# An opening without cross-partition reductions on GpSimd, and with unread products of the identity on TensorE

## The chip, the core and the metric

The kernel runs on one core of a Trainium2 chip. The metric is the time on the device in microseconds; lower is better. One profiled execution of the kernel before gives every duration below.

## The reference

One transformer block with adaptive layer norm, on x of shape (2, 2048, 512):

```python
mod = (_silu(L0_c) @ L0_wmod).reshape(L0_c.shape[0], 6, 1, -1)
sa, ca, ga, sb, cb, gb = (mod[:, 0], mod[:, 1], mod[:, 2], mod[:, 3], mod[:, 4], mod[:, 5])
ga = (2 * (ga >= 0) - 1) * jnp.maximum(jnp.abs(ga), 0.25)      # gb likewise
h = _layernorm(x, axis=-1) * (1 + ca) + sa
x = x + ga * _L0_attn_ref(h, ...)     # linear attention: 16 heads of 32, elu(q)+1, elu(k)+1
h = _layernorm(x, axis=-1) * (1 + cb) + sb
x = x + gb * _L0_ffn_ref(h, ...)      # silu(gate) * up, 1376 wide; weights are lut[idx], 16 entries
return x
```

## The kernel before, in words

x is cut into 8 groups of 512 rows (4 tiles of 128). Every engine has its own instruction stream, in an order written out by hand, and the streams meet only in semaphores. A float32 operand of a big product is kept as two float16 parts, so that a product of 128x128 by 128x512 becomes three float16 products (`three`, L1128 to L1130). To cut a matrix so, the kernel needs its largest absolute value over all 128 partitions, rounded to a power of two: VectorE reduces along the columns (`absmax`, L765), GpSimd reduces over the partitions (`all_max` with `partition_all_reduce`, L456), and VectorE makes scales from it (`pow2`, `weight`, L757 to L780).

There are three parts. **Opening**: load x, the weights of k, v and q and the six slices of `wmod`; layer norm of group 0 (`norm` on GpSimd, L462 to L468, then ScalarE L687); the maxima `S_LUT`, `S_K`, `S_H1`, `S_V`, `S_Q`; `columns` (L1281) makes the scale and shift of a layer norm as columns, with 16 products of two columns for each slice; `row` (L1290) makes the four gates as full rows of 128 equal partitions; ScalarE writes h of group 0 in four chunks (L592, L593), and GpSimd its low part (L478). **Stages A**, 0 to 7, one for each group g, each of 12 steps o: q, k and v of group g on TensorE (`out_a`, 12 products for each step), the sums kv (`kv_a`, L1178), transposes of group g+1 (`xT_a`, L1136), and on VectorE, besides its part of all that, the look-up of feed-forward weights (`lookup`, L885 to L893), two wide units in stages 0, 2, 3 and 4 and one in stage 1. Stage 0 also has `h2_columns` and `h2_scales` at steps 3 and 5, with the maximum `S_H2`. Stages 6 and 7 build M, the product of the attention sums and the output weights, for batch 0, with the maximum `S_M0`. **Stages B**, 0 to 7: gate and up of the feed-forward, slot by slot (j from 0 to 10), with the attention output of the next group between; stage B1 builds M of batch 1 with the maximum `S_M1` (`m_max`, `m_scale`). In slot (0, 10) TensorE waits for `gu_ready`, which VectorE raises behind its last look-ups of stage B1 (L906). At the end come the eight groups' down products.

All loads go through the one queue of SyncE, in the order of the program.

Of the kernel before, what the change touches and what calls it, by code (L numbers as in the profile page):

```python
# [32 lines left out]
RMAX = bass.bass_isa.ReduceOp.max  # L33

P = 128
# [60 lines left out]
def adaln_kernel(nc, x, qwT, qb, kwT, kb, vwT, vb, owT, ob, lut, gateT, upT, downT, cT, wmod, out):  # L96
    with ExitStack() as ctx:
# [58 lines left out]
        silu_cr = hid_f[:, :, :].rearrange("p i (k m) -> p (i k) m", k=KC).rearrange("p (k b) m -> p k b m", k=KC)  # L156
# [15 lines left out]
        qn_f = sb("qn_f", [P, 2, GROUP], F32)  # L172
        kv = sb("kv", [P, BATCHES, KC, P + 1], F32)
# [15 lines left out]
        mods = part(look_flat, at + 16, F32, 4, KC, BATCHES)  # L189
# [20 lines left out]
        def sems(names):  # L210
# [3 lines left out]
        c_in, lut_in, rows_in = sems("c_in lut_in rows_in")  # L214
# [4 lines left out]
        consts, silu_done, rep_done, cols_done, rows_done, rows_read = sems(  # L219
            "consts silu_done rep_done cols_done rows_done rows_read")  # L220
        maxed, reduced, dve_step, pool_step, h1_ready, v_ready, q_ready, obga_ready, w_split = sems(
            "maxed reduced dve_step pool_step h1_ready v_ready q_ready obga_ready w_split")
# [62 lines left out]
        ROW_BANK, COL_BANK = (4, 5, 0, 1), (7, 0)  # L285
# [8 lines left out]
        def _(sp):  # L294
# [7 lines left out]
            load_mod(1)  # L302
            load_mod(0)
            sp.dma_start(xg[:, 0], xv[0]).then_inc(x_in[0], 16)
            sp.dma_start(raw[0], chunked(kwT)).then_inc(raw_in[0], 16)
            load_mod(2)
            sp.dma_start(raw[1], chunked(vwT)).then_inc(raw_in[1], 16)
            for row, src in ((kb_row[:], kb), (vb_row[:], vb), (obga[:, 0], ob), (obga[:, 1], ob)):
                sp.dma_start(row, src.partition_broadcast(P)).then_inc(rows_in, 16)
            sp.dma_start(qb_col, qb).then_inc(rows_in, 16)  # L310
            sp.dma_start(raw[2], chunked(qwT)).then_inc(raw_in[2], 16)
            load_mod(5)
            sp.dma_start(xg[:, 1], xv[1]).then_inc(x_in[1], 16)
            load_mod(4)
            load_mod(3)

# [6 lines left out]
            for i in range(3):  # L323
# [3 lines left out]
            sp.wait_ge(rows_done, 4)  # L327
            sp.wait_ge(cols_done, 2)
            sp.wait_ge(consts, 3)
            for j in range(6, FC):  # L330
                load_gate_up(j, idx_in[3])
            def stage_a(g, par, load):
# [94 lines left out]
        def _(pool):  # L427
# [4 lines left out]
            def link(ins):  # L432
# [5 lines left out]
            link(pool.memset(ident[:], 0.0))  # L438
            link(pool.affine_select(out=ident[:], in_=ident[:], compare_op=ALU.not_equal, fill=1.0, base=0,
                                    pattern=[[-1, P]], channel_multiplier=1))  # L440
            link(pool.memset(head_sum[:], 0.0))
            for i in range(P // HEAD):
                link(pool.memset(head_sum[HEAD * i:HEAD * i + HEAD, COPIES * i:COPIES * i + COPIES], 1.0))
            link(pool.memset(head_out[:], 0.0))
            for c in range(KC):
                link(pool.affine_select(out=head_out[:].rearrange("p (i d) -> p i d", d=HEAD), in_=head_out[:].rearrange("p (i d) -> p i d", d=HEAD),
# [986 lines left out]
```

## Time and profile before

| | |
|---|---|
| median of 3 runs | 1290.37 us (1290.29 to 1292.86) |
| the profiled execution | 1292.91 us, its span 1291.1 us |
| TensorE busy | 1188.0 us, 92% |
| VectorE busy | 745.4 us, 58% |
| ScalarE, GpSimd busy | 392.3 us (30%), 356.6 us (28%) |

The span is from the first to the last instruction; the execution's own time holds 1.8 us more that lie around it. Times in the rows below count from the start of the span.
### The profile page before, as it was taken

To read this page: it belongs to the slowest core of one execution; us is meant where nothing else is said; L and a number is where in the kernel's file an instruction comes from. 1 tells how busy PE (TensorE), PEld (TensorE's weight loads), DVE (VectorE), ACT (ScalarE), POOL (GpSimd) and SP (SyncE) were. 2 spreads that over 40 slices of the span, in tenths; PEclk is the share of its full clock that TensorE was granted. 3 is DMA by queue.
4 is the path that set the end of the run, shared out by engine and by line. 5 is a ranking of instruction groups with operands and counts; after the bars stand their busy time and mean duration, and the time that the engine had idled before them with its cause. 6 is when DMAs were issued, how large, how long until landed. Compare 5 with 4: busy or idle time off the path is not lost.

```text
span 1291.1 us, 14367 instructions
## 1 busy us (share of the span) xinstructions
PE 1188.0 (92%) x5528; PEld 569.4 (44%) x5528; DVE 745.4 (58%) x1106; ACT 392.3 (30%) x608; POOL 356.6 (28%) x344
## 2 busy tenths in 40 slices
PE   4499699889999798796999999999999999999998
PEld 4255345444554343342444444444444444444443
DVE  2449789998856467976788698987621110010010
ACT  0224355645663532313233242433223210000000
POOL 1101000000030533525355263644523221111111
PEclk9889899999999899898999999999999999999999
DMA  9413111121201342121032131212121244444441
GB/s 326 130 33 110 66 65 35 64 98 66 74 25 65 119 165 99 57 90 66 29 107 80 66 106 72 77 69 106 39 106 48 77 179 153 153 153 153 153 153 65
DMA packets 52229, 125.79 MB, mean 97 GB/s; under 512 B 5216, under 2 KB 15456, under 8 KB 47040
## 3 DMA queue, kind: packets, MB, share of 16 engines
q1 hardware_dynamic: 52160, 124.87, 27.7%
q8 instruction: 43, 0.70, 0.2%
q14 instruction: 26, 0.21, 0.0%
HBM read 77.15 MB, written 47.71 MB: 97 GB/s over the span
## 4 chain that ended last, share of the span: by engine, by line
PE 64%; DVE 16%; issue 11%; ACT 4%; POOL 4%; DMA 1%; POOLq 0%; SPq 0%; DVEq 0%; ACTq 0%
PE bank L1128 20%; PE bank L1129 20%; PE bank L1130 20%; DVE look_buf L893 3%; DVE w_ffn L893 2%; DVE look_buf L890 1%; DVE arena L890 1%; PE bank L1247 1%; PE bank L1136 1%; DVE qp L921 1%; DVE shared L912 1%; ACT h L592 1%; ACT h_f L593 1%; DMA xg<-in_x 1%; PE bank L1281 1%
## 5 line engine op out<-in xcount | busy, mean ns | idle before, releaser
L1128 PE MATMUL bank<-h,w_ffn 128*128 128x512 f16 (+1 forms) x528 | 203.3, 385 | 23.8 <-DVEq L906 12.5
L1129 PE MATMUL bank<-h,w_ffn 128*128 128x512 f16 (+1 forms) x528 | 202.8, 384 | 0.0
L1130 PE MATMUL bank<-h,w_ffn 128*128 128x512 f16 (+1 forms) x528 | 202.4, 383 | 0.0
L544 POOL TENSOR_TENSOR shared<-hid_f,shared 128x512 f16<-128x512 f32 (+1 forms) x88 | 112.7, 1281 | 311.8 <-ACT shared L716 311.8
L1062 DVE SCALAR_TENSOR_TENSOR hid_f<-bank,sc,shared 128x512 f32<-128x512 f32 (+1 forms) x88 | 65.8, 748 | 151.2 <-PE bank L1130 114.1
L1069 DVE SCALAR_TENSOR_TENSOR shared<-bank,sc,gb_row 128x512 f32<-128x512 f32 x32 | 24.0, 751 | 215.6 <-PE bank L1130 215.6
L1128 PE MATMUL bank<-w_ffn 128*128 128x512 f16 (+1 forms) x352 | 136.3, 387 | 0.9 <-DVE hid_f L1062 0.9
L716 ACT ACTIVATE shared<-hid_f 128x512 f16<-128x512 f32 (+1 forms) x88 | 55.4, 630 | 267.1 <-DVE hid_f L1062 267.1
L1129 PE MATMUL bank<-w_ffn 128*128 128x512 f16 (+1 forms) x352 | 136.2, 387 | 0.0
L1130 PE MATMUL bank<-w_ffn 128*128 128x512 f16 (+1 forms) x352 | 136.2, 387 | 0.0
L1128 PE MATMUL bank<-arena,h 128*128 128x512 f16 x256 | 101.4, 396 | 7.9 <-issue 6.5
L1129 PE MATMUL bank<-arena,h 128*128 128x512 f16 x256 | 100.9, 394 | 0.0
L1130 PE MATMUL bank<-arena,h 128*128 128x512 f16 x256 | 100.8, 394 | 0.0
L709 ACT ACTIVATE shared<-bank,sc 128x512 f32<-128x512 f32 (+1 forms) x88 | 60.3, 685 | 127.7 <-PE bank L1130 127.7
L890 DVE TENSOR_SCALAR look_buf<-look_buf,tab_x,tab 128x512 uint32<-128x512 uint32 x133 | 98.1, 767 | 0.8
L1128 PEld LDWEIGHTS bank<-h,w_ffn 128*128 128x128 f16 (+1 forms) x528 | 53.4, 101 | 95.9 <-issue 18.5
L581 POOL TENSOR_TENSOR xg<-xg,shared 128x512 f32<-128x512 f32 x32 | 41.0, 1280 | 198.1 <-DVE shared L1069 198.1
L1130 PEld LDWEIGHTS bank<-h,w_ffn 128*128 128x128 f16 (+1 forms) x528 | 53.6, 102 | 62.8 <-issue 3.1
L462 POOL TENSOR_SCALAR sc<-mv 128x4 f32<-128x4 f32 x16 | 6.6, 410 | 266.7 <-DVE mv L803 146.4
L1129 PEld LDWEIGHTS bank<-h,w_ffn 128*128 128x128 f16 (+1 forms) x528 | 53.5, 101 | 58.7 <-issue 2.4
L893 DVE COPY_PREDICATED look_buf<-look_buf 128x512 uint32<-128x512 uint32 x76 | 71.7, 944 | 1.1
L1128 PE MATMUL bank<-arena,w_ffn 128*128 128x512 f16 (+1 forms) x176 | 66.8, 379 | 0.0
(183 smaller groups left out, 2029.5 us busy)
## 6 DMA issues: line engine op xcount, KB each, us to landing
hid_dram<-shared SPq DMA_DIRECT2D x80, 256.0 KB, 2.0
w_ffn<-hid_dram SPq DMA_DIRECT2D x8, 2560.0 KB, 9.6
xg<-in_x SPq DMA_DIRECT2D x16, 1024.0 KB, 7.2
qp_dram<-qp SPq DMA_DIRECT2D x8, 1024.0 KB, 4.9
x_dram<-xg SPq DMA_DIRECT2D x8, 1024.0 KB, 4.1
xg<-x_dram SPq DMA_DIRECT2D x8, 1024.0 KB, 4.8
out<-xg SPq DMA_DIRECT2D x7, 1024.0 KB, 11.4
qp<-qp_dram SPq DMA_DIRECT2D x6, 1024.0 KB, 5.2
```

Source lines behind the costliest of these rows:

```text
L544: pool.tensor_tensor(hid[0:m, e % HIDS, 1], hid_f[0:m, e % 2], hid[0:m, e % HIDS, 0], ALU.subtract).then_inc(hid_done, 1)
L581: pool.tensor_tensor(xg[:, par, t], xg[:, par, t], y_t[:, t % 2], ALU.add).then_inc(y_done, 1)
L592: act.activation(dst[:, 0, c], bank[c % 2][:], ACT.Identity, bias=bias, scale=scale)
L709: act.activation(silu_g[0:m, e % 2], bank[2 + 2 * (e % 2)][0:m], ACT.Silu, scale=c1(C_INV_G)[0:m]).then_inc(silu_g_done, 1)
L716: act.activation(hid[0:m, e % HIDS, 0], hid_f[0:m, e % 2], ACT.Copy).then_inc(hid_hi_done, 1)
L890: ins = dve.tensor_scalar(buf(dst), buf("m0"), tab_x[:, a:a + 1], tab[:, 2 * a:2 * a + 1], ALU.bitwise_and, ALU.bitwise_xor)
L893: ins = dve.copy_predicated(buf(dst), buf(a), buf(b))
L1062: dve.scalar_tensor_tensor(hid_f[0:m, i], bank[3 + 2 * i][0:m], c1(C_HID)[0:m], silu_g[0:m, i], ALU.mult, ALU.mult).then_inc(hid_f_done, 1)
L1069: dve.scalar_tensor_tensor(y_t[:, t % 2], bank[2 + t][:], c1(C_INV_D), gb_row[:, g // PER_BATCH], ALU.mult, ALU.mult).then_inc(y_read, 1)
L1128: pe.matmul(dst, a_hi, b_hi, start=first, stop=False)
L1129: pe.matmul(dst, a_hi, b_lo, start=False, stop=False)
L1130: last = pe.matmul(dst, a_lo, b_hi, start=False, stop=end)
```

## The change

GpSimd makes no reduction over partitions any more. In its place (`all_max` on TensorE) one product with the identity spreads the 128 per-partition maxima over a PSUM tile, and VectorE reduces it (`amax`). The maximum of the look-up table, which is the same on every partition, needs neither.

The scale and shift of a layer norm come as rows: `small_rows` runs products of 32 weight columns in strips of the array, `mod_turn` transposes the result. The gates are made in stage A1 (`g_rows`, then `row`), not in the opening. The loads have a new order: x of group 0, the weights of k, `wmod` slices 1 and 0, the weights of v and q; look-up indices are loaded between the later slices. Stage A0 takes its transposes two steps later (`M_LATE`). The first step of stage A0 waits for h chunk by chunk. `kv` is cleared by GpSimd, and `m_scale(1)` stands three slots earlier. Last, `fill` issues products of the identity with itself, into a bank that nobody reads before it is overwritten: 64 at the very start, 8 before `mod_turn(0)`, 8 before stage A0.

```diff
+            sp.dma_start(xg[:, 0], xv[0]).then_inc(x_in[0], 16)
+            sp.dma_start(raw[0], chunked(kwT)).then_inc(raw_in[0], 16)
+            load_mod(1)
+            load_mod(0)
+            sp.dma_start(raw[1], chunked(vwT)).then_inc(raw_in[1], 16)
+            sp.dma_start(raw[2], chunked(qwT)).then_inc(raw_in[2], 16)
+            load_row(kb_row[:], kb).then_inc(rows_in, 16)
+            sp.dma_start(qb_col, qb).then_inc(rows_in, 16)
+            load_two(0)
+            sp.dma_start(xg[:, 1], xv[1]).then_inc(x_in[1], 16)
+            load_mod(4)
+            load_mod(3)
+            load_two(1)
+            load_mod(2)
+            load_mod(5)
+            load_two(2)
+            load_row(vb_row[:], vb).then_inc(late_in, 16)
+            for b in range(BATCHES):
+                load_row(obga[:, b], ob).then_inc(late_in, 16)
+            sp.wait_ge(mrows_done, 1)
+            for j in range(6, FC - 1):
                 load_gate_up(j, idx_in[3])
+
...
+                if g == 1:
+                    sp.wait_ge(g_done, 1)
+                    sp.wait_ge(consts, 3)
+                    load_gate_up(FC - 1, idx_in[3])
...
-            def all_max(n, count):
-
-                pool.wait_ge(maxed, count)
-                pool.partition_all_reduce(c1(C_AMAX + n), c1(C_MAX + n), P, RMAX).then_inc(reduced, 1)
-                pool.wait_ge(reduced, count)
...
+            link(pool.memset(kv[:].rearrange("p b k n -> p (b k n)"), 0.0))
...
+            norm(0, stats_done, ve_done, rstd_done, nmr_done)
+            link(pool.memset(head_out[:], 0.0))
...
-            all_max(S_LUT, 1)
-            norm(0, stats_done, ve_done, rstd_done, nmr_done)
-            all_max(S_K, 2)
-            all_max(S_H1, 3)
-            all_max(S_V, 4)
             for c in range(KC):
                 h_lo_a(0, 0, c)
-            pool.wait_ge(h_done, 8)
-            all_max(S_Q, 5)
-
-            def h2_max():
-                pool.wait_ge(xn_done, 4 * 1 + 4)
-                all_max(S_H2, 6)
...
+            def amax(n, count, src):
+
+                dve.wait_ge(reduced, count)
+                dve.tensor_reduce(c1(C_AMAX + n), src, AX.X, ALU.max).then_inc(amax_done, 1)
+                dve.wait_ge(amax_done, count)
+
             def weight(i, n, count, col):
 
 
-                dve.wait_ge(reduced, count)
+                amax(n, count, bank[6][:, 0:P])
...
+            def mod_rows(i, n):
+
+                rows = 2 * HEAD
+                dve.wait_ge(mrows_done, i + 1)
+                dve.tensor_scalar(mod_row[i][0:rows], bank[MROW_BANK[i]][0:rows], head_sum[0:rows, 0:1], None, ALU.add).then_inc(mrow_done, 1)
+                dve.wait_ge(mrow_done, i + 1)
+                dve.tensor_reduce(c1(C_MAX + n)[0:rows], mod_row[i][0:rows], AX.X, ALU.max, apply_absolute_value=True).then_inc(maxed, 1)
...
-            stage_a(0, 0, True, LOOK_A[0], {3: [h2_columns], 5: [h2_scales]})
+            stage_a(0, 0, True, LOOK_A[0], {4: [lambda: mod_rows(1, S_H2)], 5: [h2_scales]}, M_LATE)
...
-                        8: [lambda: m_scale(1)], 9: [lambda: m_cut(1, 0), lambda: m_cut(1, 1)],
+                        5: [lambda: m_scale(1)], 9: [lambda: m_cut(1, 0), lambda: m_cut(1, 1)],
...
+                if g == 0 and o == 0:
+                    for k, pair in enumerate(pairs):
+                        pe.wait_ge(h_done, 4 + k + 1)
+                        last = three(bank[2][:], [pair], k == 0, k == KC - 1)
+                    last.then_inc(proj_done, 1)
+                else:
+                    three(bank[2 + o % 4][:], pairs).then_inc(proj_done, 1)
...
+                if c == 0 and n == 2:
+                    pe.wait_ge(amax_done, N_M1)
...
+            def all_max(count, n, dst, rows=P):
+
+                pe.wait_ge(maxed, count)
+                pe.matmul(dst, c1(C_MAX + n)[0:rows].to_broadcast([rows, P]), ident[0:rows, 0:rows], start=True, stop=True).then_inc(reduced, 1)
+
+            def small_rows(dst, tiles, done):
+
+                for k in range(KC):
+                    for i, (weights, m) in enumerate(tiles):
+                        if k == 0:
+                            pe.wait_ge(mod_in[m], 16)
+                        last = pe.matmul(dst[HEAD * i:HEAD * i + HEAD], weights(k), mod_raw[m][:, k], start=(k == 0), stop=(k == KC - 1),
+                                         tile_position=(0, HEAD * i), skip_group_check=True)
+                last.then_inc(done, 1)
...
+            def mod_turn(i):
+                rows = 2 * HEAD
+                pe.wait_ge(mrow_done, i + 1)
                 for c in range(KC):
...
+                    last = pe.transpose(bank[MCOL_BANK[i]][:, c * rows:(c + 1) * rows], mod_row[i][0:rows, c * P:(c + 1) * P], ident[0:rows, 0:rows])
+                last.then_inc(mcols_done, 1)
...
+            def g_rows():
+                pe.wait_ge(h_f_done, 4 + 3 + 4)
+                small_rows(bank[0], [(lambda k, b=b: silu_r[:, k * BATCHES + b], m) for m in (2, 5) for b in range(BATCHES)], g_done)
...
+                pe.matmul(bank[(i + 1) % 2][:], head_out[rows], g_row[rows], start=True, stop=True,
+                          tile_position=(HEAD * i, 0)).then_inc(rows_done, 1)
...
+            def fill(n):
+
+                for _ in range(n):
+                    pe.matmul(bank[3][:, 0:P], ident[:], ident[:], start=True, stop=True)
+
             pe.wait_ge(pool_step, 2)
+            fill(64)
+            all_max(N_K, S_K, bank[6][:, 0:P])
+            pe.wait_ge(rep_done, 2)
+            mod_rows(0, 1, 0)
             xT_a(0, 0, 0)
             xT_a(0, 0, 1)
-            pe.wait_ge(rep_done, BATCHES * KC)
-            row(0, 2)
+            fill(8)
+            mod_turn(0)
+            mod_max(0, N_H1, S_H1)
             xT_a(0, 0, 2)
+            all_max(N_V, S_V, bank[6][:, 0:P])
             xT_a(0, 0, 3)
-            row(1, 2)
-
...
+            fill(8)
+
+            def h2_rows():
+                pe.wait_ge(h_f_done, 4 + 3)
+                mod_rows(1, 4, 3)
+
+            def h2_turn():
+                pe.wait_ge(h_f_done, 4 + 4)
+                mod_turn(1)
+                mod_max(1, N_H2, S_H2)
+
+            stage_a(0, 0, True, {3: [h2_rows], 5: [h2_turn]}, M_LATE, first=True)
+            pe.wait_ge(pool_step, 10 + P // HEAD)
+            stage_a(1, 1, True, {0: [g_rows], 2: [lambda: row(0), lambda: row(1)], 3: [lambda: row(2), lambda: row(3)]})
...
-                    {2: [lambda: m_turn(1)], 4: [lambda: m_prod(1, 2), lambda: m_prod(1, 3)]})
+                    {2: [lambda: m_turn(1)], 4: [lambda: m_prod(1, 2), lambda: m_prod(1, 3)], 5: [lambda: m_largest(1)]})
```

## Rows read from the trace of the kernel before

**Rows 1.** The page, part 1: busy microseconds (share) and instructions.
```profile
PE 1188.0 (92%) x5528; PEld 569.4 (44%) x5528; DVE 745.4 (58%) x1106; ACT 392.3 (30%) x608; POOL 356.6 (28%) x344
```

**Rows 2.** Windows of stages 0, 1, 2: PE, PEld, DVE, ACT, POOL busy; PEclk, DMA, GB/s.
```profile
73.20:135.90 62.70, 59.12 (x288) 33.54 (x286) 49.80 (x77) 26.43 (x40) 6.50 (x7) 0.89 0.26 74
135.90:179.10 43.20, 33.18 (x161) 18.24 (x162) 31.18 (x46) 22.82 (x35) 2.84 (x4) 0.88 0.15 49
179.10:221.50 42.40, 38.92 (x194) 20.77 (x193) 40.64 (x65) 23.51 (x36) 2.54 (x4) 0.96 0.15 50
```

**Rows 3.** Timeline of GpSimd: start, us, operation, [idle before <-releaser].
```profile
31.29 0.19 POOL L462 TENSOR_SCALAR sc<-mv 128x4 f32<-128x4 f32 x1 [15.46 <-issue]
...
33.11 0.20 POOL L468 TENSOR_TENSOR sc<-sc 128x4 f32<-128x4 f32 x1
...
56.56 2.26 POOL L478 TENSOR_TENSOR h<-h_f,h 128x512 f16<-128x512 f32 x2 [7.08 <-issue]
...
148.57 0.44 POOL L462 TENSOR_SCALAR sc<-mv 128x4 f32<-128x4 f32 x1 [47.23 <-issue]
...
428.20 0.38 POOL L462 TENSOR_SCALAR sc<-mv 128x4 f32<-128x4 f32 x1 [41.70 <-issue]
```

**Rows 4.** Source lines 439 and 462: GpSimd's configuration instructions, first and last start.
```profile
L439 POOLq MODIFY_POOL_CONFIG  x2: 8/10/11, 1.9 to 2.0; - x2
...
L439 POOL TENSOR_SCALAR_AFFINE_SELECT ident<-ident x1: 291/291/291, 2.1 to 2.1; 128x128 f32<-128x128 f32 x1
...
L462 POOLq MODIFY_POOL_CONFIG  x6: 11/11/11, 20.5 to 139.0; - x6
```

**Rows 5.** Timeline of VectorE in the opening.
```profile
20.24 2.25 DVE L765 TENSOR_REDUCE sc<-w_ffn 128x1 f32<-128x2048 f32 x1
40.00 0.15 DVE L757 TENSOR_SCALAR sc<-sc 128x1 f32<-128x1 f32 x1 [17.51 <-POOL sc L456]
...
42.08 2.35 DVE L774 SCALAR_TENSOR_TENSOR arena<-w_ffn,sc,arena 128x2048 f16<-128x2048 f32 x1
...
68.12 0.15 DVE L757 TENSOR_SCALAR sc<-sc 128x1 f32<-128x1 f32 x1 [11.68 <-POOL sc L456]
...
73.25 2.47 DVE L800 BATCH_NORM_STATS2 stats<-xg 128x6 f32<-128x512 f32 x4 [0.25 <-DVE sc L842]
...
96.89 0.17 DVE L785 TENSOR_SCALAR look_buf<-bank 128x8 f32<-128x8 f32 x1 [11.71 <-PE bank L1281]
```

**Rows 6.** Timeline of TensorE, opening, and prices of its small products.
```profile
7.47 13.79 PE L1281 MATMUL bank<-look_buf,w_ffn 128*128 128x2 f32 x64 [7.47 <-DMA w_ffn<-in_wmod]
...
61.92 0.59 PE L1128 MATMUL bank<-arena,h 128*128 128x512 f16 x1 [6.50 <-issue]
...
66.97 3.60 PE L1290 MATMUL bank<-w_ffn,hid_f 128*128 128x512 f32 x8
...
372.35 1.06 PE L1178 MATMUL bank<-shared 128*128 128x129 f32 x8
...
449.18 1.06 PE L1230 MATMUL bank<-w_ffn,head_sum 128*32 128x512 f32 x8
```

**Rows 7.** Windows, 12 to 16 us: the last column is GB/s.
```profile
12.00:16.00 4.00, 4.00 (x21) 4.00 (x20) 0.13 (x1) 0.00 (x0) 0.38 (x1) 1.00 1.05 391
```

**Rows 8.** Timeline of ScalarE, first operation of the first chunk.
```profile
46.62 0.78 ACT L592 ACTIVATE h<-bank,modm 128x512 f16<-128x512 f32 x1 [10.35 <-DVEq L832]
```

**Rows 9.** Timeline of TensorE, places behind the two late maxima.
```profile
436.33 1.09 PE L1136 MATMUL bank<-ident,w_ffn 128*128 128x128 f32 x8 [2.50 <-POOL w_ffn L503]
...
579.71 0.60 PE L1136 MATMUL bank<-ident,arena 128*128 128x128 f32 x4
...
613.37 0.66 PE L1128 MATMUL bank<-h,w_ffn 128*96 128x512 f16 x1 [12.46 <-DVEq L906]
```

**Rows 10.** Timeline of VectorE around the second late maximum.
```profile
580.37 1.27 DVE L1009 SCALAR_TENSOR_TENSOR qn_f<-qp,bank 128x512 f32<-128x512 f32 x2
...
609.03 0.15 DVE L757 TENSOR_SCALAR sc<-sc 128x1 f32<-128x1 f32 x1 [8.21 <-POOL sc L456]
```

More of the change, by code:

```diff
@@ L300, in load_mod, with load_row @@
                 sp.dma_start(mod_raw[m], chunked(wmod[:, m * HID:(m + 1) * HID])).then_inc(mod_in[m], 16)
[L302 to L315, printed above, removed]
+            def load_row(row, src):
+                return sp.dma_start(row, src.partition_broadcast(P))
             def load_gate_up(j, s):
@@ L321, in load_gate_up, with load_two @@
                     sp.dma_start(ffn_idx[:, j, w, :, 0:m], chunked(src[:, j * P:j * P + m])).then_inc(s, 16)
-            for i in range(3):
+            def load_two(i):
                 sp.wait_ge(w_split, i + 1)
@@ L980, in m_scale @@
             def m_scale(b):
-                dve.wait_ge(reduced, 7 + b)
+                amax(S_M0 + b, N_M0 + b, bank[0][:, 0:P])
                 pow2(S_M0 + b)
@@ L1186, in stage_a @@
                     out_a(g, par, o)
+                    if first and o == 1:
+                        all_max(N_Q, S_Q, bank[6][:, 0:P])
                     if first and o == 3:
-                        pe.wait_ge(maxed, 3)
+                        pe.wait_ge(amax_done, N_Q)
                     if o in (3, 5, 7, 9):
@@ L1272, in t_piece @@
                 turn(xn2_of[n], c, x2T_done)
-            def columns(slot, s):
-                pe.wait_ge(mod_in[s], 16)
-                for c in range(KC):
-                    at = (slot % 2 * KC + c) * BATCHES
-                    for k in range(KC):
-                        last = pe.matmul(bank[COL_BANK[slot // 2]][:, at:at + BATCHES], mod_raw[s][:, k, c * P:(c + 1) * P], silu_c[:, k],
-                                         start=(k == 0), stop=(k == KC - 1), skip_group_check=True)
-                if slot % 2:
-                    last.then_inc(cols_done, 1)
@@ L1286, in row @@
-            def row(i, s):
-                pe.wait_ge(mod_in[s], 16)
-                for k in range(KC):
-                    last = pe.matmul(bank[ROW_BANK[i]][:], silu_cr[:, k, i % 2], mod_raw[s][:, k],
-                                     start=(k == 0), stop=(k == KC - 1))
-                last.then_inc(rows_done, 1)
-            pe.wait_ge(silu_done, 1)
-            columns(0, 1)
-            columns(1, 0)
+            def all_max(count, n, dst, rows=P):
+                pe.wait_ge(maxed, count)
+                pe.matmul(dst, c1(C_MAX + n)[0:rows].to_broadcast([rows, P]), ident[0:rows, 0:rows], start=True, stop=True).then_inc(reduced, 1)
@@ new lines, in mod_rows @@
+            def mod_rows(i, scale, shift):
+                small_rows(bank[MROW_BANK[i]], [(lambda k: silu_m[:, k], scale), (lambda k: silu_m[:, k], shift)], mrows_done)
+            def mod_turn(i):
+                rows = 2 * HEAD
+                pe.wait_ge(mrow_done, i + 1)
+                for c in range(KC):
+                    last = pe.transpose(bank[MCOL_BANK[i]][:, c * rows:(c + 1) * rows], mod_row[i][0:rows, c * P:(c + 1) * P], ident[0:rows, 0:rows])
+                last.then_inc(mcols_done, 1)
@@ L1316, in _ @@
-            for g in range(1, 5):
+            fill(8)
[9 more added lines that the diff above has]
+            stage_a(1, 1, True, {0: [g_rows], 2: [lambda: row(0), lambda: row(1)], 3: [lambda: row(2), lambda: row(3)]})
@@ L1317, in _ @@
+            for g in range(2, 5):
                 stage_a(g, g % 2, True)
```

173 lines of the change are left out of this document (86 added, 87 removed).

## Prediction

> **What bounds the kernel now.** I read the page first: TensorE is busy for 92% of the span [rows 1], so in most of the kernel only less TensorE work would help. But the change is mostly in the opening, and there the slices show TensorE little occupied. So I took the timelines of all engines for the first 160 us, then the windows by stage. In the opening everybody waits for GpSimd, and GpSimd waits for nothing that the profile shows: its first layer-norm operation starts at 31.29 [rows 3], though its configuration instruction stood at 20.5 [rows 4], so 10.8 us pass with no work. The same blank is there in front of the first low part of h, 7.1 us [rows 3], and in front of the layer norms at 148.57 (configuration at 139.0, so 9.6 us) and 428.20. Each lies where GpSimd goes from `partition_all_reduce` to ordinary operations, or back. VectorE pays: 17.51 us idle before the k weights, 11.68 before the q weights [rows 5]. So the big products start at 61.92 and VectorE's stage 0 at 73.25, while all 1 MB loads could have been in by then: the first lands at 7.5 [rows 6], and at 391 GB/s [rows 7] each further one takes 2.7 us.
>
> From stage 0 to stage 4 VectorE with its look-ups sets the pace: it is busy 40.6 of 42.4 us in stage 2. In stage 1 it is busy for only 31.2 of 43.2 us [rows 2], since that stage has half the look-ups and GpSimd's blank of 9.6 us. In stage 0 it stands for 11.7 us behind `columns` [rows 5]. Behind stage B1 it is TensorE, apart from one wait of 12.46 us at 613 [rows 9]. Everything is one chain, so what is saved before a point arrives at the end.
>
> **The opening, step by step.** x lands at 7.5, k at 10.2, `wmod` 1 and 0 at 12.9 and 15.6, v at 18.3, q at 21. An ordinary GpSimd operation came 0.1 us behind a configuration instruction at 2.0 [rows 4], and the new GpSimd stream has no reduction, so I price its first norm at its own 2.0 us (31.29 to 33.31 [rows 3]): ready at about 12.5, normalised by ScalarE at 16 (four operations of 0.78 [rows 8]). Neither is the last to arrive.
>
> That is `fill(64)`. The identity is ready at 2.4 [rows 4]. One float32 product of 128 columns is two instructions; eight such took 1.06 us at the full clock [rows 6], 0.11 to 0.13 each, twice that at half. In the kernel before, dense products ran at half clock from 61.92 to 66.97 (twelve in 5.05 us) and at full clock from there on [rows 6]. So of 128 instructions about 20 take the first 5 us and 108 take 12 to 14: the end is at 19 to 21.5; I take 19.5. If the clock never rose it would be 30 to 35. The k maximum has been waiting since 12.5, so the fill costs some 4 us of the opening against having none, but there is room for it.
>
> Then VectorE: k weights, from 40.00 to 44.43 in rows 5, so 4.4 us, and 0.3 for the new reduction: 24.5. Meanwhile TensorE makes the rows of scale and shift: eight products in two strips. Four in four strips took 1.06 us, four of full width 3.60 [rows 6]; bounds 2.1 and 7.2, I take half of serial, 3.6: 23.4. Two operations of VectorE on them, transposes, maximum, and nine tiny operations: 28. That is `h1_ready`, which ScalarE awaited until 46.62 [rows 8]. Four chunks at about 1.35 us each, and 1.15 for the last low part (half of 2.26 [rows 3]), bring h to 34.6. VectorE goes on: v maximum 2.25, v weights 4.7, q maximum 2.25 (37.2). The q maximum's product stands on TensorE behind the first two steps of stage 0, which take 2.6 us each at full clock and 5.1 at half: it comes at 38 to 43, I take 40. With 4.7 and 0.8 for the q weights and what follows, stage 0 of VectorE starts at 45.5 (43 to 48.5) where it started at 73.25: 27.7 us earlier.
>
> **Stage 0** took 62.7 us. The 11.7 us behind `columns` go; new are two operations of 512 columns, a reduction and some waiting for the rows' products, 1.5. It takes 52.5, ends at 98 instead of 135.9: 37.9 us.
>
> **Stage 1** loses GpSimd's 9.6 us but gets the gates. TensorE was busy 38.9 us in stage 2 [rows 2], a stage of the same work. `g_rows` adds 16 products in four strips, 0.27 each by rows 6, so 4.2; the four `row` products at most 0.9 each, 3.6. Together 46.7, of which it begins about 5 before VectorE's stage (when the last low part is there, a look-up share and the statistics earlier). So TensorE now bounds this stage at 41.7 us, against 43.2: 1.5 us, and most of what the blank's end gave is spent on the gates. Bounds: 38 (cheap `row` products) and 51.9 (strips serial, 14.4 instead of 4.2). Running gain 39.4.
>
> **The two late maxima.** Without the first, the norm at 428.20 is early and TensorE's wait of 2.50 us [rows 9] shrinks, but ScalarE is still in the q activations until about 436: 1 us (0 to 2.5). Without the second, VectorE's idle 8.2 us before 609.03 [rows 10] are gone, and the small operations behind it stand elsewhere, 0.95: the last look-ups are done 9.2 earlier, TensorE resumes at 604, and after so short a pause needn't run at half clock. Against that, a new wait: the transposes at 579.71 [rows 9] must now come behind VectorE's `amax`, which follows its operations at 580.37 to 581.64 [rows 10], some 2.2 us; behind it is queued the rest of slot 6. It is partly absorbed, because the pause at 613 doesn't go entirely. I take 9 (7 to 11).
>
> Sum: 27.7 + 10.2 + 1.5 + 1 + 9 = 49.4. From the profiled execution's 1292.9 that is 1243.5; the median of the runs is 2.5 below it, hence 1241.
>
> **Where the Trainium skill has a say.** The price of `g_rows` hangs on strips overlapping; rows 6 show a quarter of the serial price. The Trainium skill, "TensorEngine Tiling (Array Packing)", says in its overview that 32-column work goes up to four times as fast, and under "Key Properties" that a change of the tiling mode drains the engine. By the first `g_rows` would be an estimated 3.6 us, by the second every change between full and strip products pays a little; both stay inside my bounds.
>
> **Rivals.**
> 1. The fill doesn't do its work on the clock, or what it gives is lost before it counts. After the fill TensorE still waits for h between 26 and 31 and around 32 to 34. In the kernel before, each such pause was followed by a stretch at half clock: the pause of 6.50 us before 61.92 [rows 6], the one of 12.46 before 613.37 [rows 9]. If the clock stays low during the fill itself, it ends 13 us later and so does all that follows: 1254 to 1258. The Trainium skill, "TensorE: Matmul & The Clock Gate", Part 1, has the default state throttled and lets activity release it; by this the fill does raise the clock, and the pauses behind it take it back.
> 2. Strips run serially for float32: `g_rows` +10, the two `mod_rows` +3.6 each: about 1256. Rows 6 speak against it.
> 3. Stage 0 doesn't stay at VectorE's pace: the chain rows, copy, transposes, maximum, scales now runs from step 3 to step 5 with two engines waiting for each other, and stage 0's transposes come two steps later, so that h of group 1 is late. 5 to 10 us are lost: 1248. Nothing in the trace prices it; TensorE has about 40 us of work in a stage of 52.
> 4. It goes better: full clock for the first steps and short `row` products: 1232.
> 5. Slower than before: each product of the fill waits until the one before has written the same bank. It stands ahead of everything, so its price goes straight to the end: from 1.0 us for each of the 64 products (50 us more than I count) the gain is gone. A single instruction of this size lasts under 0.6 us with its drain (four in 0.60 [rows 9]), so this would be 1295 only if a product took five times what it does anywhere in the trace.
>
> **Numbers.** Forecast 0.60, rival 1 0.12, 2 0.07, 3 0.11, 4 0.08, 5 0.02. The forecast's own terms give 1233 to 1250; to hold 8 in 10 the range reaches to most of rival 3 and the near side of 1: 1230 to 1255. A difference under 0.2% can't be told from none. Faster 0.97, same 0.01, slower 0.02.
>
> **What the new profile would show.** GpSimd without a blank in front of a first operation, and no configuration instruction behind the first; the fill's 128 instructions ending near 19.5, clock 1.0 in their second half; `h1_ready` near 28; VectorE's stage 0 from about 45.5, stage 1 from 98, stage 2 from about 140 (179.1 before); TensorE with a wait of some 2 us at the transposes of stage B1 and 3 us or less at its slot (0, 10). What would make me wrong most easily: a fill at half clock, or stage 0 over 57 us.

## The result, and the profile after

The changed kernel takes 1248.25 us in the median (1247.88 to 1252.34, 4 runs), the kernel before 1291.01 beside it (4 runs). The ratio is 0.9677, 95% interval 0.9659 to 0.9695. Forecast were 1241, with a range of 1230 to 1255: the time lies in the range, 7 us above the forecast. The profiled execution is the one of 1252.34 us, its span 1250.5: 40.6 us less than before. It is the longest of the four, so the medians lie 42.8 us apart.

The page after, part 1 and the first line of part 4, the chain that ended last (before it was PE 64%, DVE 16%, issue 11%, POOL 4%; "issue" is time in which an engine waited for nothing that the profile shows):

```profile
PE 1181.1 (94%) x5622; PEld 563.8 (45%) x5622; DVE 750.6 (60%) x1105; ACT 393.0 (31%) x609; POOL 352.3 (28%) x337
...
PE 73%; DVE 13%; issue 6%; ACT 4%; POOL 2%; DMA 1%; POOLq 0%; SPq 0%; DVEq 0%; ACTq 0%
```

Source line 464 of the changed kernel, its configuration instructions (answers to [rows 4]):

```profile
L464 POOLq MODIFY_POOL_CONFIG  x2: 11/11/11, 1.7 to 1.7; - x2
```

The timeline of GpSimd in it (answers to [rows 3]):

```profile
10.70 0.20 POOL L454 TENSOR_SCALAR sc<-mv 128x4 f32<-128x4 f32 x1 [6.38 <-DVE mv L812]
...
29.74 2.41 POOL L486 TENSOR_TENSOR h<-h_f,h 128x512 f16<-128x512 f32 x2 [14.87 <-ACT h_f L584]
...
103.49 0.43 POOL L454 TENSOR_SCALAR sc<-mv 128x4 f32<-128x4 f32 x1 [50.81 <-DVE mv L812]
...
386.68 0.19 POOL L454 TENSOR_SCALAR sc<-mv 128x4 f32<-128x4 f32 x1 [42.15 <-DVE mv L1024]
```

All four rows of before that have a bracket ended with "<-issue". Now each names the instruction whose result GpSimd needed, and one configuration at 1.7 us is all. The first norm starts at 10.70, not at 31.29.

The prediction did not name the first blank of before, the one ahead of the maximum of the look-up table. VectorE waited for it too, and only then took the statistics of x and the k maximum (20.24 in [rows 5], 10.41 now). VectorE's timeline of before:

```profile
15.87 0.15 DVE L757 TENSOR_SCALAR sc<-sc 128x1 f32<-128x1 f32 x1 [9.42 <-POOL sc L456]
```

VectorE's timeline in the opening, which answers to [rows 5]:

```profile
10.41 2.25 DVE L763 TENSOR_REDUCE sc<-w_ffn 128x1 f32<-128x2048 f32 x1
19.37 0.29 DVE L768 TENSOR_REDUCE sc<-bank 128x1 f32<-128x128 f32 x1 [6.71 <-PE bank L1300]
...
26.35 0.23 DVE L768 TENSOR_REDUCE sc<-bank 128x1 f32<-128x64 f32 x1 [0.87 <-PE bank L1300]
...
33.46 3.12 DVE L778 SCALAR_TENSOR_TENSOR arena<-w_ffn,sc,arena 128x2048 f16<-128x2048 f32 x1
36.51 1.10 DVE L784 SCALAR_TENSOR_TENSOR sc<-sc 128x1 f32<-128x1 f32 x1
...
41.32 0.29 DVE L768 TENSOR_REDUCE sc<-bank 128x1 f32<-128x128 f32 x1 [1.28 <-PE bank L1300]
...
46.79 2.47 DVE L809 BATCH_NORM_STATS2 stats<-xg 128x6 f32<-128x512 f32 x4 [0.25 <-DVE sc L846]
```

The longest idle time is now 6.71 us, in front of the k maximum, and it ends when the fill ends. TensorE's timeline shows that, and the new products (answers to [rows 6]):

```profile
2.13 16.97 PE L1344 MATMUL bank<-ident 128*128 128x128 f32 x128 [2.13 <-POOL ident L464]
18.94 0.39 PE L1300 MATMUL bank<-ident,sc 128*128 128x128 f32 x2
19.26 3.63 PE L1308 MATMUL bank<-w_ffn,hid_f 128*32 128x512 f32 x16
...
31.80 3.26 PE L1344 MATMUL bank<-ident 128*128 128x128 f32 x16
...
99.62 3.64 PE L1308 MATMUL bank<-w_ffn,hid_f 128*32 128x512 f32 x32
...
108.47 1.13 PE L1338 MATMUL bank<-hid_f,head_out 32*128 32x512 f32 x4
```

The windows of stages 0, 1 and 2 after, columns as in [rows 2]:

```profile
46.80:100.50 53.70, 37.57 (x187) 18.95 (x190) 51.20 (x78) 24.09 (x36) 2.54 (x4) 0.90 0.35 97
100.50:142.80 42.30, 42.30 (x233) 21.36 (x226) 31.04 (x46) 25.92 (x41) 3.63 (x6) 1.00 0.15 51
142.80:185.20 42.40, 38.94 (x194) 20.45 (x193) 40.63 (x65) 23.49 (x36) 2.54 (x4) 0.96 0.18 60
```

Stage 0 lost 9 us while VectorE's work in it grew by 1.4; in stage 1 TensorE is busy without a gap, so it sets the pace there (the experiment on the gates tests this). The late places, first in TensorE's timeline (answers to [rows 9]):

```profile
402.96 0.96 PE L1136 MATMUL bank<-ident,w_ffn 128*128 128x128 f32 x4 [2.71 <-ACT h_f L584]
...
548.88 0.63 PE L1136 MATMUL bank<-ident,arena 128*128 128x128 f32 x4 [1.89 <-DVE sc L768]
...
572.62 0.42 PE L1128 MATMUL bank<-h,w_ffn 128*96 128x512 f16 x1 [2.51 <-DVEq L906]
```

and VectorE's last look-ups of stage B1 (beside [rows 10]):

```profile
566.55 0.99 DVE L890 TENSOR_SCALAR look_buf<-look_buf,tab_x,tab 128x512 uint32<-128x512 uint32 x2
567.57 3.26 DVE L893 COPY_PREDICATED look_buf<-look_buf 128x512 uint32<-128x512 uint32 x2
570.87 1.64 DVE L893 COPY_PREDICATED w_ffn<-look_buf 128x512 uint32<-128x512 uint32 x1
```

**Where the 40.6 us are.** The differences between the starts of the same instruction in both traces add up. VectorE's stages 0, 1 and 2 start 26.5, 35.4 and 36.3 us earlier (46.79, 100.52 and 142.81; before 73.25, 135.92 and 179.12); so the opening gives 26.5, stage 0 8.9, stage 1 0.9. From there to the first feed-forward product (443.97, now 408.40) the gain falls back by 0.7, to 35.6; from that to TensorE's restart in slot (0, 10) (613.37, now 572.62) come 5.2. Behind it 677.9 us are left, before 677.7. The opening changed in several things at once (the reductions, the order of the loads, rows instead of columns for scale and shift, the fill). Only the reduction and the fill were tested by themselves; what the new order of the loads is worth alone is not shown.

### The profile page after: what moved, and what is told of

Same layout as the page of the kernel before. It is cut to its first block, busy times and chain, and to the rows that moved or that the text cites. A ratio compares the mean times of both kernels' runs of the same rounds, so it can differ in the third digit from the quotient of the medians.

```text
span 1250.5 us, 14524 instructions
## 1 busy us (share of the span) xinstructions
PE 1181.1 (94%) x5622; PEld 563.8 (45%) x5622; DVE 750.6 (60%) x1105; ACT 393.0 (31%) x609; POOL 352.3 (28%) x337
## 4 chain that ended last, share of the span: by engine, by line
PE 73%; DVE 13%; issue 6%; ACT 4%; POOL 2%; DMA 1%; POOLq 0%; SPq 0%; DVEq 0%; ACTq 0%
PE bank L1128 22%; PE bank L1129 22%; PE bank L1130 22%; DVE look_buf L893 3%; PE bank L1344 2%; DVE w_ffn L893 1%; PE bank L1136 1%; PE bank L1190 1%; PE bank L1266 1%; ACT h L583 1%; PE bank L1308 1%; ACT h_f L584 1%; DVE look_buf L890 1%; DMA xg<-in_x 1%; DVE qp L921 1%
## 5 line engine op out<-in xcount | busy, mean ns | idle before, releaser
L1128 PE MATMUL bank<-h,w_ffn 128*128 128x512 f16 (+1 forms) x528 | 204.0, 386 | 13.9 <-POOL h L516 11.4
L1128 PE MATMUL bank<-arena,h 128*128 128x512 f16 x256 | 98.3, 384 | 6.4 <-issue 4.6
L707 ACT ACTIVATE shared<-bank,sc 128x512 f32<-128x512 f32 (+1 forms) x88 | 60.3, 685 | 132.7 <-PE bank L1130 132.7
L1129 PE MATMUL bank<-arena,h 128*128 128x512 f16 x256 | 98.2, 384 | 0.0
L1130 PE MATMUL bank<-arena,h 128*128 128x512 f16 x256 | 97.9, 382 | 0.0
L1130 PEld LDWEIGHTS bank<-h,w_ffn 128*128 128x128 f16 (+1 forms) x528 | 53.7, 102 | 63.4 <-issue 4.0
L1129 PEld LDWEIGHTS bank<-h,w_ffn 128*128 128x128 f16 (+1 forms) x528 | 53.7, 102 | 59.3 <-issue 3.5
```

The lines of the kernel that those rows point to most:

```text
L707: act.activation(silu_g[0:m, e % 2], bank[2 + 2 * (e % 2)][0:m], ACT.Silu, scale=c1(C_INV_G)[0:m]).then_inc(silu_g_done, 1)
L1128: pe.matmul(dst, a_hi, b_hi, start=first, stop=False)
L1129: pe.matmul(dst, a_hi, b_lo, start=False, stop=False)
L1130: last = pe.matmul(dst, a_lo, b_hi, start=False, stop=end)
```

## The experiments

All times called measured are medians; single profiles are named as such; ratios are against the kernel before, run beside. Edits are against the changed kernel unless said otherwise.

### Is it the reduction on GpSimd?

**One reduction put back**, of a column of constants, ahead of the first norm. All entries of the column are equal, so that it changes nothing in what is computed. (A semaphore count of TensorE goes up by one with it, which is not shown.)

```diff
+            link(pool.partition_all_reduce(half[:, 0:1], half[:, 0:1], P, bass.bass_isa.ReduceOp.max))
             norm(0, stats_done, ve_done, rstd_done, nmr_done)
```

> The changed kernel with one reduction over the partitions put back on GpSimd, of a column of constants, directly ahead of the norm of group 0; nobody reads its result anew. My theory: GpSimd's blanks are the price of going to this operation and back. The reduction can't start before about 14 (9.5 us behind its configuration instruction), the norm not before about 24.5 (10.8 behind); the normalised x comes at 29.5 instead of 15.7, TensorE's first transposes at 30 instead of 22.8, and the time is 6 to 8 us longer than the changed kernel's: 1254 to 1256. Rival: the norm's blank in the kernel before came from something else in that queue, and an operation of 0.4 us costs nothing: 1248.

Measured: 1261.25 us, ratio 0.9770 (0.9756 to 0.9785): 13.0 us above the changed kernel's 1248.25, and 11.4 above the median of all its eight executions (1249.8, see the last part). The timeline of GpSimd in it:

```profile
13.39 0.38 POOL L473 PARTITION_ALL_REDUCE sc<-sc  x1 [8.87 <-issue]
22.75 1.18 POOL L454 TENSOR_SCALAR sc<-mv 128x4 f32<-128x4 f32 x1 [8.97 <-issue]
```

An operation of 0.38 us brings two blanks of 8.9 us, one on the way to it and one on the way back, and the configuration instructions stand at 4.5 and 14.0, where they begin. So going to the reduction and coming back is the cause of the blanks, by one edit alone. In the kernel before, the reductions at 44.96 and 49.13, which follow the one at 39.58 with nothing else between them, waited only for VectorE: the blank comes with the change of operation, and not with each reduction. The Trainium skill, "GPSIMD Engine Reference", section 2.1, gives about 6 us for the first call of newly loaded code, and no visible instruction for it. The trace agrees that nothing is visible, but has 8.87 and 8.97 here and 5.89 to 10.8 before. The price was more than I expected. VectorE's stage 0 starts at 55.39, 8.6 us later than in the profile beside the result; the wait goes on to TensorE, as its timeline there shows:

```profile
28.76 1.97 PE L1137 MATMUL bank<-ident,xg 128*128 128x128 f32 x8 [6.13 <-ACT xg L683]
30.52 3.47 PE L1345 MATMUL bank<-ident 128*128 128x128 f32 x16
```

Behind 6.13 us without work these instructions run at half clock (eight in 1.97; eight take 1.09 at 22.82 in the changed kernel). The few us of the medians' difference beyond the 8.6 lie behind the start of stage 0 and are not located.

**The late maxima alone**: the kernel before, with only the maxima of M of both batches made on TensorE and VectorE. The core of the edit against before:

```diff
-                dve.wait_ge(reduced, 7 + b)
+                amax(S_M0 + b, 1 + b, bank[0][:, 0:P])
...
-                        8: [lambda: m_scale(1)], 9: [lambda: m_cut(1, 0), lambda: m_cut(1, 1)],
+                        5: [lambda: m_scale(1)], 9: [lambda: m_cut(1, 0), lambda: m_cut(1, 1)],
```

> The kernel before with nothing but the maxima of M for both batches taken by TensorE and VectorE, at the places of the changed kernel. The prediction gave these two 10 us: 1281. The two traces give 4.7 (minus 0.5 at the first, plus 5.2 at the second): 1286.3.

Measured: 1283.0 us, ratio 0.9945 (0.9927 to 0.9964), span 1281.1. The stretch from stage 6 to the first feed-forward product has 96.7 us in both: the first maximum gives nothing. From there to slot (0, 10) it is 161.8 instead of 169.4: the second gives 7.6 in this trace, 5.2 in the changed kernel. Both times TensorE waits 2.5 us at the end of it. Another 2.7 us of this profile's gain stand ahead of stage 6, where the two kernels are the same: that is how much two profiles can differ by themselves.

### Why does the second late maximum give less?

**The last bias additions a slot later.** In the changed kernel `xob` runs on GpSimd beside VectorE's last look-ups of stage B1.

```diff
-                        before[9] = [lambda: xob(n + 1, 1 - par)]
+                        before[10 if s == 1 else 9] = [lambda: xob(n + 1, 1 - par)]
```

> The changed kernel with GpSimd's four additions of the output bias for group 3 (6.5 us, from 568.5 on) one slot later in stage B1. My theory: they now fall on VectorE's last look-ups ahead of gu_ready, which take 5.9 us where they took 3.3 in the kernel before, since the two engines slow each other; this is what ate most of the second maximum's gain. One slot later the look-ups end at 570, TensorE's pause of 2.51 us and half a stretch at half clock go: 3 to 4 us less, 1244 to 1245. Rival: the look-ups are slow for another reason, or the collision only moves to the cuts of M: 1248.

Measured: 1248.72 us (1244.60 to 1249.08), ratio 0.9663 (0.9641 to 0.9685). No difference that the times can tell, against 3 to 4 us expected, but the trace shows the mechanism. GpSimd's timeline in the kernel before, around the second late maximum:

```profile
608.62 0.38 POOL L456 PARTITION_ALL_REDUCE sc<-sc  x1 [5.91 <-issue]
616.11 5.68 POOL L496 TENSOR_TENSOR xg<-xg,obga 128x512 f32<-128x512 f32 x4 [7.11 <-issue]
```

VectorE's last look-ups fell between the two there:

```profile
611.01 1.49 DVE L893 COPY_PREDICATED look_buf<-look_buf 128x512 uint32<-128x512 uint32 x2
612.53 0.73 DVE L893 COPY_PREDICATED w_ffn<-look_buf 128x512 uint32<-128x512 uint32 x1
```

GpSimd's timeline in the changed kernel:

```profile
568.52 6.49 POOL L504 TENSOR_TENSOR xg<-xg,obga 128x512 f32<-128x512 f32 x4
```

VectorE's timeline with the additions later, where the rows at 567.57 and 570.87 stood:

```profile
567.82 2.34 DVE L893 COPY_PREDICATED look_buf<-look_buf 128x512 uint32<-128x512 uint32 x2
570.20 0.73 DVE L893 COPY_PREDICATED w_ffn<-look_buf 128x512 uint32<-128x512 uint32 x1
```

and TensorE's in the same kernel:

```profile
571.04 0.42 PE L1128 MATMUL bank<-h,w_ffn 128*96 128x512 f16 x1 [0.69 <-DVEq L906]
```

The copy at 570 takes 0.73 us instead of 1.64, the two before it 2.34 instead of 3.26 (in the kernel before, 1.49, with GpSimd idle), and TensorE waits 0.69 instead of 2.51. From its restart to the end it has 676.3 us here, and 677.9 in the changed kernel. The same two values stand in every profile of the changed kernel's versions: 676.3 in the three where TensorE waits 0.7 us there, 677.9 to 678.0 where it waits 2.5 or more. So the collision costs 1.8 us ahead of this point and 1.6 behind it, 3.4 in all; the medians do not show them, and what happens at the other pauses varies by as much from one execution to the next (last part). GpSimd, while it stood in its blank, had left VectorE alone; freed, it slows it. Part of the collision only moves on: with the additions later, two of VectorE's operations that cut M take 1.37 us each, where 0.48 and 0.43 is their time alone (L990, L991). The Trainium skill, "SBUF — State Buffer", "Who interferes with whom", has a VectorE instruction with two inputs from SBUF contend with a GpSimd instruction that reads SBUF. The trace agrees in kind: this copy's time more than doubles.

**The scale of M later.** Two versions without the fill, with the gates early and `xob` late, differ only in where VectorE makes M's scale: in slot 5 as the changed kernel does, or ahead of `hid_full(5)`, which ends the wait of 1.89 us at the transposes.

```diff
-                        5: [lambda: m_scale(1)], 9: [lambda: m_cut(1, 0), lambda: m_cut(1, 1)],
+                        9: [lambda: m_cut(1, 0), lambda: m_cut(1, 1)],
...
-                    early={4: [lambda: m_out(1, 0), lambda: m_out(1, 1)]})
+                    early={4: [lambda: m_out(1, 0), lambda: m_out(1, 1)], 5: [lambda: m_scale(1)]})
```

With the scale moved:

> No fill, gates at the end of A0, bias additions one slot later, and m_scale(1) ahead of the product of slot 5 instead of behind it (so that TensorE's transposes don't wait 1.9 us for it). If the parts add up: 2 + 2 + 3 + 1 us below the changed kernel: 1240. Rival: they hide behind the same waits, and the sum is no more than the best of them: 1245.

With the scale where it was:

> As the combined version without fill (gates at step 11 of stage A0, the last bias additions a slot later), but m_scale(1) stands where the changed kernel has it. If the move of m_scale was worth nothing because the wait at slot (0, 10) grew by what the wait at the transposes lost: 1242 to 1243, wait at the slot back at some 1 to 2.5 us. If the move was good for its 1.9 us: 1244.

Measured: moved, 1242.39 us (ratio 0.9625, 0.9611 to 0.9640); left alone, 1237.87 (0.9595, 0.9582 to 0.9608). The move loses, by intervals that just miss each other. TensorE's timeline with the scale moved:

```profile
561.67 0.63 PE L1128 MATMUL bank<-h,w_ffn 128*96 128x512 f16 x1 [4.77 <-DVEq L906]
```

and with the scale left alone:

```profile
539.79 0.63 PE L1136 MATMUL bank<-ident,arena 128*128 128x128 f32 x4 [1.89 <-DVE sc L768]
...
561.71 0.42 PE L1128 MATMUL bank<-h,w_ffn 128*96 128x512 f16 x1 [0.69 <-DVEq L906]
```

Though the first passed the transposes 4.1 us earlier (535.66 against 539.79), both restart at 561.7: VectorE there waits 4.24 us for ScalarE (L707). The wait was moved, and after the long one the first product takes 0.63 and not 0.42: half clock. To the end it is 677.9 us then, 676.3 otherwise. The rest of the difference of the medians is not located in these two profiles.

### The gates

**`g_rows` at step 11 of stage A0**, into the pause of 4.58 us that TensorE has there, instead of step 0 of stage A1.

```diff
-            stage_a(0, 0, True, {3: [h2_rows], 5: [h2_turn]}, M_LATE, first=True)
+            stage_a(0, 0, True, {3: [h2_rows], 5: [h2_turn], 11: [g_rows]}, M_LATE, first=True)
...
-            stage_a(1, 1, True, {0: [g_rows], 2: [lambda: row(0), lambda: row(1)], 3: [lambda: row(2), lambda: row(3)]})
+            stage_a(1, 1, True, {2: [lambda: row(0), lambda: row(1)], 3: [lambda: row(2), lambda: row(3)]})
```

> The changed kernel with g_rows at the end of stage A0 instead of behind the first step of A1, all else the same. My theory: TensorE bounds A1 because it has the gates there, while it stands idle for 4.58 us at the end of A0 and then runs its next 12 products at half clock. Moved, the 3.64 us lie in that pause, and the clock stays up: A1 ends 3.6 to 5.5 us earlier, 1243 to 1245. Rival: A1 is set by the chain of k_bias, exponential and kp_out between ScalarE and VectorE, and the gates don't matter: 1248.

Measured: 1247.56 us, ratio 0.9660 (0.9644 to 0.9676), against 1243 to 1245 expected, and not clear of the changed kernel. Windows of its stages 0 and 1:

```profile
46.60:102.10 55.50, 43.96 (x221) 21.68 (x222) 51.45 (x79) 24.69 (x37) 2.54 (x4) 0.88 0.33 94
102.10:139.40 37.30, 37.30 (x195) 19.70 (x194) 31.65 (x47) 25.33 (x40) 4.18 (x6) 1.00 0.17 57
```

Stage 1 falls from 42.3 to 37.3, stage 0 grows by 1.8: stage 2 starts 3.4 us earlier. So stage 1 is bounded by TensorE's work, as predicted. Stage 2 starts at 139.36, against 142.81 and 142.17 in the two profiles of the changed kernel; from there to the end this profile takes 1107.3 us and those 1107.7 and 1104.2, so that the gain is as large as what two profiles of one kernel differ by.

### What does the fill do?

**No fill**: the three calls of `fill` (80 products) removed.

> The changed kernel without any of its 80 unread products. My theory: the 64 hold the k maximum from 12.7 to 19.0 us, but what then bounds is the scale and shift rows, which can't start before wmod slice 0 has landed at about 15.6; without the fill they run at half clock, 7.3 instead of 3.6 us, and end at 23, where they end now. So h1_ready stays within 1.5 us of 28.05 and the time within 2 us of the changed kernel: 1247 to 1250. Rival: the fill is worth what it seems to be for, a fast clock up to stage 0; then without it everything from the rows to step 1 of stage 0 is at half clock and the time is 1254 to 1260.

**A short fill**: 36 products, ended before the k maximum arrives, 12 behind it.

```diff
-            fill(64)
+            fill(36)
             all_max(N_K, S_K, bank[6][:, 0:P])
+            fill(12)
```

> The changed kernel with the 64 products cut to 36 ahead of the k maximum and 12 behind it. My theory: the fill ends at 11.5, the k maximum goes through at 12.9, the second part lasts until wmod slice 0 lands (15.6), the rows run at full clock to 19.3 and h1_ready comes at 24.3 instead of 28.05; stage 0 starts 3.7 us earlier and the time is 1244.5. Rival: the clock isn't up by then or drops in the short wait, the rows take 7 us and nothing is gained: 1248.

Measured: 1246.41 (ratio 0.9657, 0.9641 to 0.9673) and 1246.18 (0.9652, 0.9637 to 0.9666): both about 2 us below the changed kernel, intervals overlapping. So the changed kernel and the one without fill were run again side by side, in one group with the version of 1237.87, the changed kernel first:

> The changed kernel, unaltered, timed beside its version without the fill, so that both share their runs of the kernel before. My theory: 1246 to 1249 us, with VectorE's stage 0 from 46.8 as in its first profile, within 0.3. Whoever holds that the kernel without the fill is really faster expects these runs to lie 2 us above it again, clear of the intervals.

> The changed kernel without its 80 products of the fill, once more, in the same job. My theory, that the fill gives nothing because what it speeds up lies beside VectorE's weights and the low parts of h: within 2 us of the changed kernel, on either side, intervals overlapping. Rival 'the fill pays': over 2 us slower. Rival 'the fill costs': 2 us or more faster, stage 0 from 45.0.

and the fill was put back into the fastest version, in a later group:

> The fastest version so far (gates at step 11 of stage A0, the last bias additions a slot later, no fill: 1237.9 us, ratio 0.9595) with the 80 products of the fill put back. If the fill costs what the stage starts show, 1.5 to 2 us: 1239 to 1240, ratio 0.961. If it costs what the times of the changed kernel with and without it differ by, 5.7 us: 1243 to 1244, ratio 0.964. If the fill pays: under 1237.

| | with fill | without |
|---|---|---|
| changed kernel | 1251.84, ratio 0.9699 (0.9684 to 0.9713) | 1246.13, 0.9660 (0.9647 to 0.9673) |
| fastest version | 1243.86, ratio 0.9646 (0.9626 to 0.9665) | 1237.87, 0.9595 (0.9582 to 0.9608) |

Twice the intervals lie apart, by 5.7 and 6.0 us in the medians. In the first comparison of the changed kernel it was 1.8, and over all eight executions of each it is 3.7 (1249.8 and 1246.1). So **the fill costs some 4 to 6 us, 0.3% to 0.5%**, against my theory that it is worth nothing either way. Only about 2 us of it are located, at the start of VectorE's stage 0: it lies at 46.41 to 47.29 in the five profiles with the whole fill (the one with the reduction put back left out) and at 43.87 to 45.25 in the four without (46.8 and 44.8 in the mean). The timeline of TensorE in the changed kernel without fill:

```profile
13.01 0.77 PE L1300 MATMUL bank<-ident,sc 128*128 128x128 f32 x2 [13.01 <-DVE sc L763]
...
15.97 4.54 PE L1308 MATMUL bank<-w_ffn,hid_f 128*32 128x512 f32 x14 [0.35 <-DMA w_ffn<-in_wmod]
```

and of VectorE in it:

```profile
39.57 0.29 DVE L768 TENSOR_REDUCE sc<-bank 128x1 f32<-128x128 f32 x1 [2.96 <-PE bank L1300]
...
45.04 1.29 DVE L809 BATCH_NORM_STATS2 stats<-xg 128x6 f32<-128x512 f32 x2 [0.25 <-DVE sc L846]
```

Without it the k maximum is there at 13.8 instead of 19.4, the strips run slower (14 instructions in 4.54 instead of 16 in 3.63), the q maximum is waited for longer (2.96 instead of 1.28), and of the head start of 5.5 us some 1.4 to 1.8 are left at stage 0. So the fill's clock buys back most, but not all, of what waiting for its end costs. The rest of the price is not located: the two profiles behind the first row of the table differ by 2.0 us from end to end, and those behind the second by 6.2, of which the next part says more.

**All gains with the short fill** and the scale moved:

> As the run without fill, but with the short fill (36 and 12, and the two of 8). If unread products are good for anything, it is here, where TensorE waits less elsewhere: 1 to 2 us below the run without fill, 1238 to 1239. Rival: the same or slower.

Measured: 1242.69 us (0.9626, 0.9608 to 0.9644), against 1242.39 without any fill: my expectations that a short one would win 3 us by itself, and 1 to 2 here, were wrong. It does bring VectorE's stage 0 forward, to 43.70 and 43.97 in the two profiles with it, 3 us earlier than the long one does; but that is no earlier than the earliest profile without any.

### How much one profile can tell

The eight executions of the changed kernel fall into two groups, 1247.9 to 1248.3 and 1251.4 to 1252.5, four in each. The traces are of one each (spans 1250.5 and 1246.4). TensorE's timeline behind the same two pauses, in the longer execution:

```profile
276.62 1.89 PE L1190 MATMUL bank<-shared 128*128 128x129 f32 x8 [2.39 <-DVE shared L917]
...
467.81 1.91 PE L1266 MATMUL bank<-kb_row,head_out 32*128 32x512 f32 x4 [4.16 <-DVE kb_row L1002]
```

and in the shorter one:

```profile
275.83 1.16 PE L1190 MATMUL bank<-shared 128*128 128x129 f32 x8 [2.37 <-DVE shared L917]
...
465.92 1.46 PE L1266 MATMUL bank<-kb_row,head_out 32*128 32x512 f32 x4 [4.16 <-DVE kb_row L1002]
```

Same program, same wait of 2.4 us, once the clock is halved behind it and once not. It makes stage 5 take 43.4 or 41.8 us. Behind the wait of 4.16 us four instructions take 1.91 or 1.46 us, and 1.13 where the clock is full. So two profiles of one kernel differ by 4 us, and a difference of that size between two kernels' profiles is no gain until their times show it. The Trainium skill, "TensorE: Matmul & The Clock Gate", Part 1, says of a kernel's start that the number of its slow products varies from run to run, and gives 6, 11 and 14 for one kernel; in these traces the same shows behind a pause in mid-kernel. TensorE's timeline in the fastest version with the fill:

```profile
273.84 2.07 PE L1190 MATMUL bank<-shared 128*128 128x129 f32 x8 [2.38 <-DVE shared L917]
```

and without it:

```profile
271.37 1.16 PE L1190 MATMUL bank<-shared 128*128 128x129 f32 x8 [2.37 <-DVE shared L917]
```

The first lost its clock at this wait, the second kept it: of the 6.2 us between their spans that is 1.7. Another 2.0 stand at the start of stage 0, 0.5 in stage 0, 0.6 between stage 6 and the first feed-forward product, and 1.5 between that and slot (0, 10). Nor is this loss the fill's alone: of the four profiles without any fill two lost the clock at this wait and two kept it, of the same five with the whole fill four lost it, wholly or in part. Whether the fill makes such losses likelier, or these fell so by chance, isn't settled.

## Why the prediction was right, point by point

Right: what bounded the kernel, the size of the effect in its main terms, and the sign. Too high by 8.8 us in the sum (49.4 against 40.6 by spans; 44.7 in the second profile of the changed kernel, 42.8 by the medians). All five terms came out below their forecast: 1.2 in the opening, 1.3 in stage 0, 0.6 in stage 1, 1.7 and 3.8 at the late maxima. The cause of the blanks, which the sum takes for granted, was tested only afterwards, and holds.

- **Opening**: 27.7 forecast, 26.5 measured. The fill ended at 19.1 (19.5), the rows' 16 instructions took 3.63 (3.6), h began at 28.14 (28), the q maximum came at 41.3 (40). What I had not counted: GpSimd's low parts of h slow VectorE's v weights, L778 3.12 us instead of 2.35 and L784 1.10 instead of 0.15.
- **Stage 0**: 52.5 us forecast, 53.7 measured; gain 8.9 instead of 10.2. Rival 3 (1248) hit the time but not the way: VectorE waits only 1.19 us for the new chain of scale and shift.
- **Stage 1**: TensorE bounds it, as said; 41.7 forecast, 42.3 measured. That it came so near is partly luck. `g_rows` took 3.64 for 32 instructions (4.2 forecast for them), the four `row` products 2.3 (3.6): 1.9 less together. But behind a wait of 4.58 us TensorE's first step of the stage took 4.37 for its twelve products, nine of them at half clock, where 2.6 were counted: 1.8 more. Rival 2, serial strips, is out: 32 instructions of four strips take as long as 16 of two. (Its own terms add up to 1258, not to the 1256 that it names.) No drain shows between full products and strips: `g_rows` starts at 99.62, where the last full product (99.22, 0.46 us) ends.
- **First late maximum**: 1 forecast, 0 measured alone and -0.7 in the profile beside the result (from the start of stage 2 on), and the bound was the engine I named: the transposes now wait 2.71 us for ScalarE instead of 2.50 for GpSimd.
- **Second late maximum: the mis-sized term.** "I take 9 (7 to 11)": it was 5.2 in the profile beside the result, 7.1 in the second one, 7.6 alone. The new wait at the transposes was as forecast (1.89 us, 2.2 forecast). What failed is "the last look-ups are done 9.2 earlier": they take 5.9 us now where they took 3.3, because GpSimd's additions (`xob`) run beside them. With the additions a slot later 1.8 us come back at this point. Of the rest, 1.7 were lost behind the wait of 4.16 us at 467, where the granted clock came back later than in the second profile (0.68 in the 10 us behind it, against 0.83), which lost 0.3 there; its 7.1 and 1.8 make 8.9, near the 9 forecast, and the fastest version measures 8.7 in its profile. "Needn't run at half clock" failed too: behind the wait of 2.5 us 677.9 us are left, as many as behind the 12.46 before (677.7), and 676.3 only where the wait is 0.7.
- **Rival 1**, that the fill's clock is lost before it counts: half true. The clock did rise in the fill (its 128 instructions took 16.97 us; at the pace of half clock that the version with the reduction shows, 16 in 3.47, they would have taken 27.8), and in the windows behind the pause it is down to 0.68 at 32 to 36 us. And the fill has a price of 4 to 6 us, not a gain. I wrote that it costs some 4 us against none but that there is room; there isn't, and that line would have been the one to price.
- **Rival 5**, each product waiting for the one before: no; 0.13 us for an instruction.

## What to carry to other kernels

This GpSimd stream paid a blank each way between cross-partition reductions and ordinary operations: look for "<-issue" of 6 to 11 us in front of an operation, and count the changes from one kind to the other, not the reductions. One left by itself cost 11 to 13 us in the opening; two taken out by themselves, late in the kernel, gave 7 to 8. When an engine is freed, ask what it will run at the same time as its neighbour: here a gain of 9 us became one of 5 to 8. Warming the clock ahead of work that waited for something else gave nothing here, and cost 0.3% to 0.5%; the version without the fill, with the gates in a pause of TensorE and the additions a slot later, is the fastest of all: 1237.87 us, ratio 0.9595.

## What the runs showed of the hardware that I had not expected

- The blank is paid on the way back too: 8.87 and 8.97 us for one reduction of 0.38, and none between reductions that follow each other.
- VectorE's predicated copies of 128x512 take 0.73 us alone and 1.64 beside a GpSimd addition; its operation on a column of 128x1 went from 0.15 to 1.10.
- Four strips of 32 columns ran 32 float32 instructions in 3.64 us, two strips 16 in 3.63: the strips really overlap.
- After the same idle time of 2.4 us TensorE's clock was halved in some executions (eight instructions in 1.89 us) and not in others (1.16).
